# The stage between second attention and the expert choice, redone: 128-row projection, gate weights stationary, masks on two engines, experts' remainders spread

## The chip, the cores and the metric

One NeuronCore of one Trainium2 chip runs the whole program. The metric is the device time in microseconds (us) of one execution, and the number compared is the median over runs.

## What is computed

Two gated layers over x, 8 batches of 128 rows of 512 numbers, all in float32. The lines that matter here are the end of the second attention and the second feed-forward part, a mixture of 8 experts of which each row takes its best 2:

```python
out = jnp.einsum('de,bew->bdw', Wo, o) + bo[:, None]      # o: 64 x 128 per patch, after gelu
out = out * masks
...
x = x + tanh(g_xattn[1]) * out
h = layernorm(x)
logits = h @ W_gate + b_gate                               # 512 -> 8 experts
_, top_idx = jax.lax.top_k(logits, 2)
y_all = relu(einsum('bsd,edh->bseh', h, W_e) + b_e)
y = take_along_axis(y_all, top_idx[..., None], axis=2).mean(axis=2)
x = x + tanh(g_ffn[1]) * y
```

## The kernel before

The kernel is written by hand, one instruction stream for each engine, with semaphores between them. Each engine runs its own stream strictly in order, and that order is fixed in the code. The loops run over the 8 batches (b = 0 to 7). The stage that the change touches lies between the second attention and the experts. In this document it is called the middle stage. It starts at about 800 us of the trace and ends when the selection `sel` is there, at 842.75 us.

For each batch b the middle stage does this:

- ScalarE: `gelu(b)` in place on `o_t[0:64, b]` (L866; for b = 7 straight from PSUM, L874).
- GpSimd: `masked(b)` multiplies `o_t[0:64, b]` by the mask (L626). Row 64 of `o_t` (loaded by L403) holds the mask itself, and row 64 of `wo1g` holds the bias.
- TensorE: `output(b)` is the projection, `wo1g` (65 x 128, stationary) times `o_t[:, b]` (65 x 512, moving), into PSUM bank 2 + b % 2 (L1670). float32 matmuls are two instructions each.
- VectorE: `attended(b)` adds it to X (L1210), then `bn_stats` (L911) and `bn_aggr` (L914).
- GpSimd: `row_scale(3, b)`, three short instructions, makes the row's scale (L496 to L499).
- VectorE: `final_rows(b)` normalises the rows into `h` (L917), one or two batches later. SyncE stores them (`keep_rows`, L449). For b of 4 and more, `final_rows` waits until the first four stores have landed, since the buffers are used again.
- TensorE: `turn_last(b)`, four transposes of `h` (L1677). ScalarE: copies them to `xt` (L877).
- TensorE: `gate(b)` (L1683), with `xt` (128 x 128) stationary and `wg` (128 x 8) moving, for four k.
- VectorE: `choose(0)` for batches 0 to 3 and `choose(1)` for 4 to 7 (L1240 to L1255) make `sel`. Ahead of them it copies `tri` (L1233).

TensorE's order is `output` 0, 1, 2, and then for i = 3 to 10: `output(i)`, `turn_last(i-3)`, `gate(i-4)`. Behind `sel` come the lists of rows for each expert, the gather of rows by an indirect DMA, and 23 tiles of expert matmuls (`expert(i)`). Each expert's weights are split into a high part (`expert_hi`, ScalarE, L683) and a remainder (`expert_lo`, GpSimd L502 or VectorE L1223), four pieces for each of 8 experts, 32 in all. Before the change GpSimd makes pieces 8 to 15 behind the last `row_scale`, and VectorE makes pieces 0 to 7 behind the lists. Pieces 16 to 31 are made inside the experts' loop by both. `rows_lo(i)` (L1331) and `biased(i)` (L1338) are VectorE's other work there.

SyncE's queue loads experts 4 to 7 (L407) as soon as `ot_mm` counts the last `turn_out`, which is the turning of the attention's output (L1628), and after that it loads `route` and `tri_raw` (L452, L453), ahead of `keep_rows`.

Of the kernel before, what the change touches and what calls it, by code (L numbers as in the profile page):

```python
# [46 lines left out]
def flamingo_gated_two_layers(nc, x, ctx, ctx_t, mask_tq, mask_b, g_xattn, g_ffn, wq0, wk0, wv0, wo0,  # L47
# [6 lines left out]
    with ExitStack() as stack:  # L54
# [70 lines left out]
        wo1g = sb("wo1g", [E1 + 1, P])  # L125
# [124 lines left out]
        o_t = sb("o_t", [E1 + 1, B, D])  # L250
# [71 lines left out]
        HALF = N // 2  # L322

# [14 lines left out]
        def _(sp):  # L338
# [64 lines left out]
            sp.dma_start(o_t[E1:E1 + 1, :, :], mask_b.rearrange("b o d -> o b d")).then_inc(maskb_in, 16)  # L403
# [47 lines left out]
            sp.wait_ge(gelu_ok, CREDIT + B)  # L451
            sp.dma_start(route[:, :], c_route[:, P:]).then_inc(route_in, 16)  # L452
            sp.dma_start(tri_raw[:, :], c_route[:, 0:P]).then_inc(route_in, 16)  # L453
# [30 lines left out]
        def _(gp):  # L484
# [180 lines left out]
        def _(ac):  # L665
# [237 lines left out]
        def _(ve):  # L903
            start_counts(ve, (wo1_ok, ctl_ok, prep_v, cap_ok, stat_ok, aggr_ok, h_ok, htl_ok, rot_ok, e_ok, rec_ok, at_ok, al_ok,
                              x1_ok, bbg_ok, lg_ok, lgm_ok, lgs_ok, lgi_ok, al2_ok, zw_ok, tb_ok, hc_ok, keep_ok, pen_ok, qk_ev,
                              cv_ok, mx_ok, sb_ok, oi_ok, on_ok, x3_ok, sel_ok, rank_ok, td_ok, x4_ok, real_ok, wel_v, tri_ok,
# [270 lines left out]
            for b in range(2, B):  # L1177
                mix(b, b % 2, last=b == B - 1)
                row_stats(2, b - 2, b % 2, x2_ok)
                if b == 3:  # L1180
                    nc.vector.tensor_scalar(wo1g[:, :], wo1[:, :], tanh_g[0:E1 + 1, 1:2], None, ALU.mult).then_inc(wo1_ok, 1)
# [6 lines left out]
                if b == B - 5:  # L1188
                    ve.wait_ge(maskb_in, 16 * (B + 1))
# [42 lines left out]
            ve.wait_ge(route_in, 32)  # L1232
            nc.vector.tensor_copy(tri[:, :], tri_raw[:, :]).then_inc(tri_ok, 1)  # L1233

            def choose(half):
# [4 lines left out]
                nc.vector.tensor_tensor(gl[:, at, :], ps[:, 4 + half, 0:4 * EX].rearrange("p (b e) -> p b e", b=4),  # L1240
# [122 lines left out]
        def _(pe):  # L1363
# [441 lines left out]
```

## Time and profile before

| | us |
|---|---|
| median of 3 runs (962.52 to 968.63) | 965.4 |
| the profiled execution, whole | 966.84 |
| its span in the trace | 965.0 |
| granted TensorE clock, mean over the span | 0.952 of full |
| TensorE matmuls busy in the span | 894.5 (93%) |
| VectorE, ScalarE, GpSimd busy | 619.6, 325.0, 404.5 |
| middle stage, 801.2 to 842.75 | 41.55 |

Times inside the kernel are read from the trace of the one profiled execution, in us from the start of its span. The 1.84 us between its span and its whole time lie around the span. A granted clock of 1.00 is 2.4 GHz and 0.50 is 1.2 GHz.

### The profile page before, as it was taken

The page shows a single profiled execution, that of the slowest core. Times are in us where ns is not written, and L with a number is a line of the kernel's source. Part 1 is how long each engine was busy: PE and PEld are TensorE (multiplying, and loading weights), DVE is VectorE, ACT ScalarE, POOL GpSimd, SP SyncE. Part 2 cuts the span into 40 slices and gives each one's busy share as a digit, 9 for nine tenths or more (in the row PEclk, how much of TensorE's full clock was granted, in tenths as well). Part 3 has the DMA queues.
Part 4 walks back from the last instruction along what each step waited for, and adds up shares of the span by engine and source line. Part 5 has one row for each costly group of instructions (what it writes and reads, how often), then busy time and mean ns, then how long its engine had stood idle before and what let it go on. Part 6 is the DMA issues. An engine that isn't in the chain of part 4 may idle for free.

```text
span 965.0 us, 13870 instructions
## 1 busy us (share of the span) xinstructions
PE 894.5 (93%) x4771; PEld 728.3 (75%) x4771; DVE 619.6 (64%) x1067; ACT 325.0 (34%) x581; POOL 404.5 (42%) x417
## 2 busy tenths in 40 slices
PE   5999999999999999999999999988999998857993
PEld 4778878978878877877977877865888885745772
DVE  5975675375674276575376577578888875777345
ACT  4333143223133214124214124221665664612230
POOL 4651532251442153253153153337764606528551
PEclk9999999999999999999999999989999996559997
DMA  9020120020120011120011011202344205313448
GB/s 314 11 88 1 33 88 1 12 87 2 33 88 1 13 45 43 33 88 1 12 43 44 1 27 52 87 26 61 113 136 134 66 2 214 142 44 131 134 149 307
DMA packets 42242, 70.13 MB, mean 73 GB/s; under 512 B 7034, under 2 KB 14779, under 8 KB 42051
## 3 DMA queue, kind: packets, MB, share of 16 engines
q1 hardware_dynamic: 37060, 56.97, 18.1%
q0 software_dynamic: 3680, 12.06, 3.8%
q8 instruction: 43, 0.70, 0.3%
q10 hardware_dynamic: 1440, 0.24, 0.1%
q14 instruction: 19, 0.16, 0.1%
HBM read 52.61 MB, written 10.22 MB: 65 GB/s over the span
## 4 chain that ended last, share of the span: by engine, by line
PE 84%; DVE 8%; issue 3%; DMA 2%; ACT 1%; ACTq 1%; POOL 1%; DVEq 0%; SPq 0%
PE ps L1370 18%; PE ps L1372 18%; PE ps L1371 17%; PE ps L1491 6%; PE ps L1483 6%; PE ps L1620 5%; PE ps L1499 3%; PE ps L1608 3%; PE ps L1601 2%; PE ps L1670 1%; DMA rows_in<-h_rows,gather_i 1%; PE ps L1716 1%; PE ps L1628 1%; DVE h L917 1%; PE ps L1576 1%
## 5 line engine op out<-in xcount | busy, mean ns | idle before, releaser
L528 POOL TENSOR_TENSOR q_t<-rot_a,rot_b 128x512 f32<-128x512 f32 x64 | 82.7, 1291 | 152.8 <-DVE rot_b L962 152.8
L960 DVE TENSOR_TENSOR rot_a<-ps,cos 128x512 f32<-128x512 f32 x80 | 55.2, 689 | 87.2 <-PE ps L1372 86.6
L1370 PE MATMUL ps<-xt_hi,wq_hi 128*128 128x512 f32 x256 | 107.6, 420 | 0.5 <-DVE rot_b L962 0.5
L1370 PE MATMUL ps<-wo_hi,at_hi 128*128 128x512 f32 x256 | 106.7, 417 | 0.4 <-DVE at_lo L1068 0.4
L1372 PE MATMUL ps<-xt_hi,wq_lo 128*128 128x512 f32 x256 | 101.1, 395 | 0.0
L1371 PE MATMUL ps<-xt_lo,wq_hi 128*128 128x512 f32 x256 | 101.0, 394 | 0.0
L1372 PE MATMUL ps<-wo_hi,at_lo 128*128 128x512 f32 x256 | 100.2, 391 | 0.0
L1371 PE MATMUL ps<-wo_lo,at_hi 128*128 128x512 f32 x256 | 99.9, 390 | 0.0
L755 ACT ACTIVATE ps<-ps 128x512 f32<-128x512 f32 x64 | 37.2, 582 | 178.6 <-PE ps L1483 178.6
L768 ACT ACTIVATE at_hi<-ps 128x512 fp32r<-128x512 f32 x64 | 38.2, 597 | 171.7 <-PE ps L1499 171.7
L1073 DVE TENSOR_TENSOR X<-ps,X 128x512 f32<-128x512 f32 x64 | 44.2, 690 | 74.0 <-PE ps L1372 73.7
L592 POOL TENSOR_TENSOR k_blk<-k,diag 96x512 fp32r<-96x512 f32 x64 | 65.4, 1053 | 24.7 <-DMA k<-qk_lo 24.7
L502 POOL TENSOR_TENSOR wq_lo<-wq_raw,wq_hi 128x512 fp32r<-128x512 f32 x32 | 41.4, 1297 | 78.8 <-ACT wq_hi L683 78.8
L1370 PEld LDWEIGHTS ps<-wo_hi,at_hi 128*128 128x128 f32 x256 | 48.0, 187 | 30.3 <-DVE at_lo L1068 17.2
L1491 PE MATMUL ps<-v_ones,e_w 128*128 128x129 f32 x512 | 67.7, 275 | 0.0
L528 POOL TENSOR_TENSOR k_t<-rot_a,rot_b 128x512 f32<-128x512 f32 x16 | 20.7, 1294 | 108.5 <-DVE rot_b L962 108.5
L1620 PE MATMUL ps<-v_pad,p_t 128*128 128x72 f32 x512 | 64.8, 269 | 1.1 <-ACT p_t L836 1.0
L1068 DVE TENSOR_TENSOR at_lo<-ps,at_hi 128x512 fp32r<-128x512 f32 x64 | 44.2, 690 | 32.6 <-ACT at_hi L768 32.6
L1483 PE MATMUL ps<-q_t,k_t 128*128 128x512 f32 x128 | 64.1, 593 | 0.0
L1491 PEld LDWEIGHTS ps<-v_ones,e_w 128*128 128x128 f32 x512 | 62.8, 192 | 0.7
L1620 PEld LDWEIGHTS ps<-v_pad,p_t 128*128 128x128 f32 x512 | 62.2, 192 | 1.4 <-ACT p_t L836 1.1
L1051 DVE TENSOR_TENSOR e_w<-ps,cap 128x512 f32<-128x512 f32 x64 | 44.1, 689 | 28.8 <-ACT ps L757 28.5
(217 smaller groups left out, 2131.2 us busy)
## 6 DMA issues: line engine op xcount, KB each, us to landing
wq_raw<-in_wq SPq DMA_DIRECT2D x8, 1024.0 KB, 5.2
wo_raw<-in_wo SPq DMA_DIRECT2D x8, 1024.0 KB, 5.1
w_raw<-in_we SPq DMA_DIRECT2D x8, 1024.0 KB, 5.7
X<-in_x SPq DMA_DIRECT2D x4, 512.0 KB, 11.9
wk_raw<-in_wk SPq DMA_DIRECT2D x8, 256.0 KB, 2.9
q_t<-in_ctx_t SPq DMA_DIRECT2D x2, 1024.0 KB, 9.5
wv_raw<-in_wv SPq DMA_DIRECT2D x4, 512.0 KB, 3.7
ctx_s<-in_ctx SPq DMA_DIRECT2D x8, 256.0 KB, 4.2
```

The source lines that it names most:

```text
L528: nc.gpsimd.tensor_tensor(dst, rot_a[:, r % 2, :], rot_b[:, r % 2, :], ALU.add).then_inc(rope_ok, 1)
L592: nc.gpsimd.tensor_tensor(k_blk[0:PARTS, b % 2, g, patch, :, :], bcast(k3[0:PARTS, g, patch * P:(patch + 1) * P].bitcast(F32), HG), diag[0 ...
L960: nc.vector.tensor_tensor(heads(rot_a[:, r % 2, :]), heads(bank), bcast(cos[:, :], 4), ALU.mult)
L1051: nc.vector.tensor_tensor(heads(e_w[:, b % 2, :]), heads(ps[:, 2 + b % 2, :]), bcast(cap[:, :], G), ALU.min).then_inc(e_ok, 1)
L1068: nc.vector.tensor_tensor(at_lo[:, b % 2, :], ps[:, 6, :], at_hi[:, b % 2, :].bitcast(F32), ALU.subtract).then_inc(al_ok, 1)
L1073: nc.vector.tensor_tensor(X[:, b, :], ps[:, 7, :], X[:, b, :], ALU.add).then_inc(x1_ok, 1)
L1370: nc.tensor.matmul(dst, w_hi, x_hi, start=start and k == 0, stop=False)
L1371: nc.tensor.matmul(dst, w_hi, x_lo, start=False, stop=False)
L1372: last = nc.tensor.matmul(dst, w_lo, x_hi, start=False, stop=stop and k == n - 1)
L1483: nc.tensor.matmul(ps[:, 2 + b % 2, :], k_t[:, b * P:(b + 1) * P], q_t[:, :, b * P:(b + 1) * P], start=True, stop=True).then_inc(s_mm, 1)
L1491: last = nc.tensor.matmul(ps[:, 4 + n // 2, at:at + P + 1], e_w[:, b % 2, n * P:(n + 1) * P], v_ones[:, b, 1 if odd else 0, 0:P + 1], star ...
L1620: last = nc.tensor.matmul(ps[:, 6 + j, patch * VA:(patch + 1) * VA], p_t[:, u % 2, n * P:(n + 1) * P], v_pad[:, at:at + VA], start=head == ...
```

## The change

- `wo1g` and `o_t` have 128 rows instead of 65. Rows 65 to 127 of `wo1g` are zeros (rows 64 to 127 by a memset, then row 64 is written over), and the mask is loaded into rows 64 to 127 of `o_t`, as 64 copies, 1 MB, later in SyncE's queue than the one row was.
- Gate: `wg` (8 columns) is stationary and `xt` (128 columns) moves. The result, 8 x 128, is copied to SBUF by ScalarE (`gate_row`) and turned back by TensorE (`gate_columns`).
- Masks 0, 1, 5 and 6 are made by VectorE, masks 2, 3, 4 and 7 by GpSimd.
- TensorE issues `output(0)` and `output(1)` ahead of the last `turn_out`.
- The order of GpSimd's stream: masks 2 to 4, then `row_scale(0)` to `row_scale(7)` with six `expert_lo` (pieces 0 to 5) and `masked(7)` between them. VectorE makes pieces 6 to 11 behind the lists and 12 to 15 behind the first `rows_lo`.
- ScalarE makes six high parts ahead of the loop and one or two in each of its rounds. The copy of `tri` moves from VectorE to ScalarE.
- `route` and `tri_raw` are loaded during the second attention, and no longer between the experts' loads and `keep_rows`.

```diff
-        wo1g = sb("wo1g", [E1 + 1, P])
+        wo1g = sb("wo1g", [P, P])
-        o_t = sb("o_t", [E1 + 1, B, D])
+        o_t = sb("o_t", [P, B, D])
+        BY_VECTOR = (0, 1, 5, 6)
+        def masks_done(b):
+            return sum(n <= b for n in BY_VECTOR), sum(n <= b for n in range(B) if n not in BY_VECTOR)
...
-            sp.dma_start(o_t[E1:E1 + 1, :, :], mask_b.rearrange("b o d -> o b d")).then_inc(maskb_in, 16)
...
+                if b == 2:
+                    sp.dma_start(o_t[E1:P, :, :], mask_b.rearrange("b o d -> o b d").to_broadcast([P - E1, B, D])).then_inc(pen_raw, 16)
                 stack(b)
...
+            for g in range(2):
+                sp.wait_ge(k3_in[g], 48 * B)
+                sp.wait_ge(q3_in[g], 48 * B)
+            sp.dma_start(route[:, :], c_route[:, P:]).then_inc(route_in, 16)
+            sp.dma_start(tri_raw[:, :], c_route[:, 0:P]).then_inc(route_in, 16)
             sp.wait_ge(ot_mm, CREDIT + B)
...
-            masked(0)
-            masked(1)
-            for b in range(2, B):
+            for b in range(2, 5):
                 masked(b)
-                if b == B - 1:
-                    nc.gpsimd.memset(ones_r[:, :].bitcast(F32), 1.0).then_inc(kz_ok, 1)
-                row_scale(3, b - 2, b % 2)
-            row_scale(3, B - 2, 0)
-            row_scale(3, B - 1, 1)
-            for n in range(2 * KT, 4 * KT):
-                expert_lo(n // KT, n % KT)
+            nc.gpsimd.memset(ones_r[:, :].bitcast(F32), 1.0).then_inc(kz_ok, 1)
+            for b in range(B):
+                row_scale(3, b, b % 2)
+                if b == 1:
+                    masked(B - 1)
+                elif b < B - 1:
+                    expert_lo(*divmod(b - min(b, 1), KT))
...
+            def gate_row(b):
+                ac.wait_ge(ot_mm, CREDIT + B + b + 1)
+                nc.scalar.activation(r_d[0:EX, b // 4, b % 4 * P:(b % 4 + 1) * P], ps[0:EX, 4 + b % 2, 0:P], ACT.Copy).then_inc(ot_ev, 1)
...
+            for n in range(6):
+                expert_hi(n // KT, n % KT)
             for b in range(B):
                 ac.wait_ge(ht_mm, CREDIT + 2 * B + b + 1)
                 nc.scalar.activation(xt[:, :, b * P:(b + 1) * P], heads(ps[:, b % 2, :]), ACT.Copy).then_inc(hth_ok, 1)
-                for n in range(2 * b, 2 * b + 2):
+                if b >= 1:
+                    gate_row(b - 1)
+                if b == B - 1:
+                    gate_row(b)
+                for n in range(6 + b + min(b, 2), 7 + b + min(b + 1, 2)):
                     expert_hi(n // KT, n % KT)
+            ac.wait_ge(route_in, 32)
+            nc.scalar.activation(tri[:, :], tri_raw[:, :], ACT.Copy).then_inc(tri_ok, 1)
...
+                    nc.vector.memset(wo1g[E1:P, :], 0.0).then_inc(wo1_ok, 1)
+                    ve.wait_ge(wo1_ok, CREDIT + 1)
...
+            masked(0)
+            masked(1)
             over_sums(B - 1, 1)
+            masked(5)
+            masked(6)
...
-            for n in range(KT + 2):
+            for n in range(6, 12):
                 expert_lo(n)
             rows_lo(0)
-            expert_lo(KT + 2)
-            expert_lo(KT + 3)
+            for n in range(12, 16):
+                expert_lo(n)
...
-                    last = nc.tensor.matmul(ps[:, 4 + b // 4, b % 4 * EX:(b % 4 + 1) * EX], xt[:, k, b * P:(b + 1) * P], wg[:, k, :],
+                    last = nc.tensor.matmul(ps[0:EX, 4 + b % 2, 0:P], wg[:, k, :], xt[:, k, b * P:(b + 1) * P],
                                             start=k == 0, stop=k == KT - 1)
-                last.then_inc(gate_mm, 1)
+                last.then_inc(ot_mm, 1)
+
+            def gate_columns(b):
+                pe.wait_ge(ot_ev, CREDIT + B - 1 + b + 1)
+                nc.tensor.transpose(ps[:, 6 + b // 4, b % 4 * EX:(b % 4 + 1) * EX], r_d[0:EX, b // 4, b % 4 * P:(b % 4 + 1) * P],
+                                    ident[0:EX, 0:EX]).then_inc(gate_mm, 1)
...
-            for b in range(3):
-                output(b, b % 2)
+            output(0, 0)
+            output(1, 1)
+            turn_out(B - 1, 1)
+            output(2, 0)
             for b in range(3, B + 3):
                 if b < B:
                     output(b, b % 2)
                 turn_last(b - 3)
                 if b >= 4:
                     gate(b - 4)
+                if b >= 5:
+                    gate_columns(b - 5)
             gate(B - 1)
+            gate_columns(B - 2)
+            gate_columns(B - 1)
```

## Rows read from the trace of the kernel before

**Rows 1.** Windows: window, its length, busy time of each engine, PEclk, DMA share, GB/s

```profile
812.00:829.00 17.00, 17.00 (x58) 12.39 (x56) 9.44 (x20) 7.75 (x15) 8.17 (x17) 0.50 0.47 178
838.50:858.20 19.70, 5.64 (x25) 5.48 (x25) 16.00 (x48) 6.59 (x13) 5.18 (x5) 0.50 0.34 124
```

**Rows 2.** Timeline of one round: start, us, engine, line, operation, tiles, count, idle before

```profile
820.56 2.05 PE L1670 MATMUL ps<-o_t,wo1g 65*128 65x512 f32 x2
822.41 1.06 PE L1677 MATMUL ps<-ident,h 128*128 128x128 f32 x4
822.65 0.69 DVE L1210 TENSOR_TENSOR X<-ps,X 128x512 f32<-128x512 f32 x1 [2.20 <-PE ps L1670]
823.26 1.71 PE L1683 MATMUL ps<-wg,xt 128*128 128x8 f32 x8
823.38 0.69 DVE L911 BATCH_NORM_STATS2 stats<-X 128x6 f32<-128x512 f32 x1
824.11 0.18 DVE L914 BATCH_NORM_AGGREGATE mean_var<-stats 128x2 f32<-128x6 f32 x1
824.22 0.55 DVE L917 TENSOR_SCALAR h<-X,mean,rstd 128x512 f32<-128x512 f32 x1
824.83 2.05 PE L1670 MATMUL ps<-o_t,wo1g 65*128 65x512 f32 x2
```

**Rows 3.** Windows in which the clock falls, stays low, is low and rises, or stays full

```profile
801.25:801.50 0.25, 0.25 (x2) 0.25 (x3) 0.00 (x0) 0.25 (x1) 0.25 (x1) 0.59 0.00 0
803.20:808.40 5.20, 5.20 (x6) 1.65 (x6) 3.03 (x6) 0.55 (x1) 1.52 (x4) 0.50 0.74 246
671.60:675.10 3.50, 3.37 (x8) 2.13 (x9) 3.40 (x8) 0.64 (x2) 0.93 (x4) 0.51 0.34 86
675.00:675.25 0.25, 0.25 (x3) 0.17 (x2) 0.25 (x1) 0.16 (x1) 0.25 (x2) 1.00 0.78 197
883.25:888.00 4.75, 2.23 (x11) 1.43 (x10) 4.70 (x5) 1.17 (x3) 4.09 (x5) 1.00 0.42 145
```

**Rows 4.** Timeline, the float32 matmul that fills half of the stretch from 671.6

```profile
672.29 1.91 PE L1576 MATMUL ps<-h,wqk 128*128 128x512 f32 x2
```

**Rows 5.** Timeline, the head of the middle stage

```profile
798.72 3.71 POOL L626 TENSOR_TENSOR o_t<-o_t,mask_bb 64x512 f32<-64x512 f32 x3 [25.23 <-ACT o_t L866]
799.03 3.22 ACT L866 ACTIVATE o_t<-o_t 64x512 f32<-64x512 f32 x6
799.18 1.11 PE L1620 MATMUL ps<-v_pad,p_t 128*128 128x72 f32 x8 [0.97 <-ACT p_t L836]
801.20 1.92 PE L1628 MATMUL ps<-ident,o_n 128*64 128x128 f32 x8 [0.91 <-DVE o_n L1152]
805.16 0.69 DVE L1210 TENSOR_TENSOR X<-ps,X 128x512 f32<-128x512 f32 x1 [4.02 <-PE ps L1670]
```

**Rows 6.** Timeline, the tail of the middle stage

```profile
829.87 10.80 POOL L502 TENSOR_TENSOR w_lo<-w_raw,w_hi 128x512 fp32r<-128x512 f32 x8
829.93 1.49 DVE L917 TENSOR_SCALAR h<-X,mean,rstd 128x512 f32<-128x512 f32 x1 [0.44 <-POOL rstd L499]
831.34 1.29 DVE L1233 CAST tri<-tri_raw 128x128 fp32r<-128x128 f32 x1
839.39 0.18 DVE L1240 TENSOR_TENSOR gl<-ps,bg 128x32 f32<-128x32 f32 x1
842.57 0.18 DVE L1255 TENSOR_SCALAR sel<-rank 128x32 fp32r<-128x32 f32 x1
```

**Rows 7.** One line of the source each: duration min/median/max in ns, when, shapes

```profile
L1424 PE MATMUL ps<-maskf,ones x2: 275/275/275, 23.6 to 23.7; 128*128 128x128 f32 x2
L877 ACT ACTIVATE xt<-ps x8: 597/597/597, 812.4 to 835.1; 128x512 f32<-128x512 f32 x8
```

**Rows 8.** Timeline, VectorE and SyncE's queue where `wo1g` and the mask rows are made ready

```profile
637.04 0.70 DVE L1181 TENSOR_SCALAR wo1g<-wo,tanh_g 65x128 f32<-65x128 f32 x1
676.32 0.52 SPq L397 DMA_DIRECT2D ctx_s<-in_ctx  x1
683.87 2.60 SPq L421 DMA_DIRECT2D k<-qk_hi  x4
```

More of the change, by code:

```diff
@@ L449, in keep_rows @@
                 sp.dma_start(h_rows[b * P:(b + 1) * P, :], (h if b % 4 < 2 else h2)[:, b % 2, :]).then_inc(hrow_out, 16)
-            sp.wait_ge(gelu_ok, CREDIT + B)
-            sp.dma_start(route[:, :], c_route[:, P:]).then_inc(route_in, 16)
-            sp.dma_start(tri_raw[:, :], c_route[:, 0:P]).then_inc(route_in, 16)
             for b in range(B):
@@ L679, in _ @@
             start_counts(ac, (ot_ev, gates_ok, hth_ok, cth_ok, wkh_ok, wvh_ok, wqh_ok, wo_hi_ok, v_ok, th_ok, ex_ok, ah_ok, wbh_ok,
-                              lge_ok, zt_ok, qkh_ok, p_ok, pt_ok, gelu_ok, weh_ok, r_ok, gh_ok))
+                              lge_ok, zt_ok, qkh_ok, p_ok, pt_ok, gelu_ok, weh_ok, r_ok, gh_ok, tri_ok))
             def hi_part(dst, raw, done):
@@ L905, in _ @@
                               x1_ok, bbg_ok, lg_ok, lgm_ok, lgs_ok, lgi_ok, al2_ok, zw_ok, tb_ok, hc_ok, keep_ok, pen_ok, qk_ev,
-                              cv_ok, mx_ok, sb_ok, oi_ok, on_ok, x3_ok, sel_ok, rank_ok, td_ok, x4_ok, real_ok, wel_v, tri_ok,
+                              cv_ok, mx_ok, sb_ok, oi_ok, on_ok, x3_ok, sel_ok, rank_ok, td_ok, x4_ok, real_ok, wel_v,
                               slot_ok, hot_ok, glo_ok, y0_ok))
@@ L1180, in _ @@
                 if b == 3:
-                    nc.vector.tensor_scalar(wo1g[:, :], wo1[:, :], tanh_g[0:E1 + 1, 1:2], None, ALU.mult).then_inc(wo1_ok, 1)
+                    nc.vector.memset(wo1g[E1:P, :], 0.0).then_inc(wo1_ok, 1)
+                    ve.wait_ge(wo1_ok, CREDIT + 1)
+                    nc.vector.tensor_scalar(wo1g[0:E1 + 1, :], wo1[:, :], tanh_g[0:E1 + 1, 1:2], None, ALU.mult).then_inc(wo1_ok, 1)
                     nc.vector.memset(q3[PARTS:PARTS + 1, :, :, :].bitcast(F32), 1.0).then_inc(pen_ok, 1)
@@ L1188, in _ @@
                 if b == B - 5:
-                    ve.wait_ge(maskb_in, 16 * (B + 1))
+                    ve.wait_ge(maskb_in, 16 * B)
                     rows(0, 0, p_w)
@@ L1204, in _, with masked @@
                 batch(b, b % 2, more=b + 2 < B, last=b == B - 1)
+            def masked(b):
+                ve.wait_ge(gelu_ok, CREDIT + b + 1)
+                nc.vector.tensor_tensor(o_t[0:E1, b, :], o_t[0:E1, b, :], mask_bb[0:E1, b, :], ALU.mult).then_inc(keep_ok, 1)
+            masked(0)
+            masked(1)
             over_sums(B - 1, 1)
+            masked(5)
+            masked(6)
             def attended(b, j):
@@ L1231, in _ @@
             final_rows(B - 1, 1)
-            ve.wait_ge(route_in, 32)
-            nc.vector.tensor_copy(tri[:, :], tri_raw[:, :]).then_inc(tri_ok, 1)
             def choose(half):
@@ L1239, in choose @@
                 ve.wait_ge(gate_mm, CREDIT + 4 * half + 4)
-                nc.vector.tensor_tensor(gl[:, at, :], ps[:, 4 + half, 0:4 * EX].rearrange("p (b e) -> p b e", b=4),
+                nc.vector.tensor_tensor(gl[:, at, :], ps[:, 6 + half, 0:4 * EX].rearrange("p (b e) -> p b e", b=4),
                                         bcast(bg[:, :], 4), ALU.add).then_inc(rank_ok, 1)
@@ L1663, in _ @@
             weighted(B - 1, 1, H1 - 1)
-            turn_out(B - 1, 1)
             def output(b, j):
-                pe.wait_ge(om_ok, CREDIT + b + 1)
+                by_v, by_p = masks_done(b)
+                pe.wait_ge(keep_ok, CREDIT + B + by_v)
+                if by_p:
+                    pe.wait_ge(om_ok, CREDIT + by_p)
                 pe.wait_ge(x3_ok, CREDIT + b - 1)
@@ L1719, in parts_done @@
             def parts_done(i):
+                if i == 0:
+                    return 0, KT
                 if i < 4:
-                    return min(i + 1, 2) * KT, max(i - 1, 0) * KT
+                    return 2 + (i - 1) * KT, 6
                 if i < EX - 1:
-                    return 2 * KT + 2 * (i - 3), 2 * KT + 2 * (i - 3)
-                return 2 * KT + 9, 2 * KT + 7
+                    return 10 + 2 * (i - 3), 6 + 2 * (i - 3)
+                return 19, 13
             def expert(i):
@@ L1730, in expert @@
                     by_v, by_p = parts_done(i)
-                    pe.wait_ge(wel_v, CREDIT + by_v)
-                    if by_p:
-                        pe.wait_ge(wel_ok, CREDIT + by_p)
+                    pe.wait_ge(wel_ok, CREDIT + by_p)
+                    if by_v:
+                        pe.wait_ge(wel_v, CREDIT + by_v)
                 pe.wait_ge(glo_ok, CREDIT + i + 1)
```

3 lines of the change are left out of this document (2 added, 1 removed).

## The prediction

> **What bounds the kernel now.** I read the windows of the middle stage first, then the timeline of one round, then the windows of TensorE's clock, and last the head and the tail of the stage. In the windows, TensorE is busy for 17.00 of 17.00 us between 812 and 829, and its clock is at the lower level, 1.2 GHz, all that time [rows 1]. VectorE is busy for 9.44, ScalarE and GpSimd for less. So in the rounds TensorE sets the pace, and it does so at half speed. The timeline shows a round of 4.27 us (820.56 to 824.83): from start to start 1.85 for the projection's two instructions, 0.85 for four transposes and 1.57 for the eight gate instructions [rows 2]. (Starts are used, since the durations shown include a tail that overlaps the next instruction.) VectorE waits 2.20 us in each round for the projection.
>
> The clock falls at 801.3 [rows 3]. Before it TensorE had been idle 0.97 us for `p_t` and 0.91 us for `o_n`, with 1.11 us of narrow matmuls between [rows 5]. Then it streams the 65-row projection without a gap from 803.2 to 808.4, 5.20 of 5.20 us, and the clock doesn't rise. At 671.6 to 675.0 it was low as well, and there it rose, after no more than 3.5 us in which TensorE was busy for 3.37 [rows 3]. Half of that stretch was a float32 matmul of 512 columns over 128 rows, 1.91 us [rows 4], and the rest 97-row matmuls and transposes. So busy time of 65 rows did not raise the clock and less busy time of 97 and 128 rows did. Between 883.25 and 888.0 TensorE was busy only 2.23 of 4.75 us, with 128 rows throughout, and the clock stayed full [rows 3]. In the rounds 1.57 of each 4.27 us are spent on gate instructions of 8 columns, in which TensorE mostly loads weights.
>
> At the end of the stage, VectorE's short instructions run beside GpSimd's eight remainders, 10.80 us in a row. `h` takes 1.49 us instead of 0.55, `tri` takes 1.29, and from the end of `h`(7) at 831.42 to the end of `sel` at 842.75 it is 11.33 us [rows 2, 6].
>
> **The change, part by part.** The sum is made on the end of `sel`, since what stands behind it (lists, gather, 23 tiles) keeps its order.
>
> *Projection of 128 rows, gate weights stationary.* At either clock the two instructions of the projection stream 512 columns as before: nothing saved by the shape itself. The gate becomes eight instructions that move 128 columns. The trace has one float32 matmul of that shape, two instructions of 275 ns each, tail included, at the full clock [rows 7]. Lower bound for the spacing: a transpose of 128 columns, a quarter of 0.85 at the lower clock [rows 2], so 107 ns at the full one. Upper bound: 275. I take the lower, as the tails overlap in rows 2 too: 8 x 107 ns, or 0.85, for a gate at the full clock and 1.71 at the lower. Now it is 1.57. `gate_columns` adds one small transpose, about 0.11 or 0.2. A round of TensorE is then half of 1.85 + 0.85, and 0.85 + 0.11, so 2.3 us at the full clock, and 4.27 + 0.14 + 0.2 or some 4.5 at the lower. (The projection's 1.85 holds 0.14 of waiting, so 4.4 is nearer, and is used.)
>
> *Which clock.* Moving columns through all 128 rows now fill projection, transposes and gate. At the lower clock that is nearly all of 4.4 us, like the stretch that rose at 675. At the full clock and VectorE's pace (below) it is 2.2 of 2.6 us, more than the 2.23 of 4.75 that kept it. I take the full clock for the rounds. Whether it falls at the head doesn't matter much: `output(0)` and `output(1)` now fill the 0.91 us gap, and if it falls all the same, TensorE streams `output(1)`, `turn_out` and `output(2)`, 1.7 + 1.9 [rows 5] + 1.7 us at the lower clock, which takes it to about 809, no later than VectorE's third addition.
>
> *Head.* ScalarE's gelus end at 799.6, 800.1, ... 802.25 (3.22 us for six) [rows 5]. GpSimd's masks take 3.71/3 = 1.24 us [rows 5]. VectorE does masks 0 and 1 before it is wanted for `o_n`. Masks 5 and 6 stand ahead of `attended(0)` in its stream, and GpSimd's masks 2 to 4 run from 800.2 to 803.9. A VectorE mask alone costs 0.69 (an addition of as many elements, [rows 2]) and beside GpSimd up to 1.49 (`h`, [rows 6]). So from 801.75, when gelu 5 is done, they end between 803.2 and 804.8. I take 804.5 for the start of `attended(0)`, against 805.16 now [rows 5]. Bounds: 803.2 to 805.5.
>
> *Rounds.* VectorE needs 0.69 + 0.69 + 0.18 us and gaps, 1.57 from start to the end of the group [rows 2]; with 0.14 to the next (an estimate) it is 1.7, and with `h` 2.25. Two rounds without `h` put `attended(2)` at 807.9. Five more lead to `attended(7)`. In each GpSimd now runs a `row_scale` (about 1.0 us, an estimate from three short instructions) and one remainder or mask of 1.24 to 1.35 [rows 5, 6]. GpSimd needs 2.4 us a round, so it is not far from setting the pace, and beside its long instruction `h` takes up to 1.49 in place of 0.55. I take a third of that, 0.3, as the mean: 2.6 a round (bounds 2.25 and 3.2), 13.0 for five, `attended(7)` at 820.9. Then come 1.7 and three `h` of 0.55: `h`(7) ends at 824.2 against 831.42, so 7.2 us earlier. `h`(4) also waits for the first four stores, which are now issued closer to it; the store of `h`(3) leaves at 818.6 and `h`(4) is due at 820.3, so a stall of 0 to 1 is inside the bounds.
>
> *Tail.* GpSimd has no remainder left, and `tri` is on ScalarE. `choose(1)` takes 3.36 us from 839.39 to 842.75 now, of which its second instruction alone stood beside GpSimd [rows 6]; without about 1.0 of this it is 2.4. `choose(0)` needs as much and runs while TensorE and ScalarE turn the last batch. From the end of `h`(7): transposes 0.65, `xt` 0.6 [rows 7], gate 1.1 behind gate 6, `gate_row` 0.3, `gate_columns` 0.3, `choose(1)` 2.4, together 5.35 against 11.33 now. Saved: 6.0. (Bounds of this saving: 4.0 if the clock is low there and each step costs 0.3 more, 6.5.)
>
> *Behind it.* TensorE waits between few matmuls from 838.5 to 858.2 at the lower clock, busy 5.64 of 19.70 [rows 1]. Its waits are as long after the change, so I take nothing there. VectorE makes four remainders behind the first `rows_lo` instead of two, in the shadow of the first tile: 0 to 1 us, I take 0. The pieces 0 to 5 that GpSimd makes early are not on VectorE's path now either, since the first tile waits for the gather. ScalarE's six high parts ahead of the loop end at about 807.3, and `xt`(0) is wanted after 810. `route` and `tri_raw` are loaded while the DMA queues are idle.
>
> *Ahead of it.* The memset of 64 rows of `wo1g` with its wait stands in front of VectorE's 0.70 us `wo1g` instruction [rows 8]. There VectorE is on the path (TensorE waits for VectorE a few instructions later). The row of the same size is 0.18 to 0.70; I take 0.3 lost. The 1 MB of mask rows goes out behind the load at 676.32. The next waiting work of SyncE comes at 683.87 [rows 8], 7 us later, which hides it; without that cover it would delay the keys of batch 2 by some 3 us.
>
> Sum: 7.2 + 6.0 - 0.3 = 12.9 us. The profiled execution took 966.84 us, its span is 965.0, so this gives a span of 952.1 and 953.9 whole. The profiled run is 1.4 above the median of 965.4, so for the median it is **952.5 us**.
>
> **The rivals.**
>
> *No change, the clock stays low in the rounds.* The gate's stationary operand has only 8 columns, and the trace doesn't show whether such a matmul counts like a wide one. If it does not, little has changed. TensorE then needs 4.4 us a round: `turn_last(0)` at 810.4 behind `h`(0), the ten steps up to gate 7 at 839.5, `gate_row` and `gate_columns` until 840.3, `choose(1)` until 842.7. That is today's 842.75. With the memset it makes **965.5**. For it: 5.20 us without a gap did not raise the clock. Against it: those had 65 rows.
>
> *Half of it.* The clock rises and falls again in turn. Rounds then are on average midway between 2.6 and 4.4, so 3.5: five rounds cost 4.5 more, and the tail about 1: **958**. Here the Trainium skill has a rule that would lead there. "TensorE: Matmul & The Clock Gate", section "Part 4: PE-mode transpose", says that transposes don't count as work that keeps the clock up. By that rule the 0.43 us of each round would fall out of the count. No row here tells it apart, as transposes never stand alone long enough.
>
> *Slower.* The gate's matmuls are dearer than I take them. At the upper bound of 275 ns a piece, eight are 2.2 us at the full clock instead of 0.85 and TensorE needs 3.6 a round, which still is less than today's 4.27. It decides only with the low clock: 550 ns a piece make a round of 7.1, and eight rounds cost 22 us: 987. The point from which it is slower by over 1% is a spacing of about 360 ns at the low clock, where 213 is seen for 128 columns.
>
> **How the numbers follow.** Full clock in the rounds: 0.60. By the bounds above (head -1.3 to +1.0, rounds -1.75 to +3, tail -0.5 to +2) its own range is 949 to 958. Half of it: 0.15. No change: 0.21. Slower: 0.04. The range 948 to 965.5 takes in the first two and half of the third. For this kernel 1% is 9.7 us, about what a measurement can tell from no change. Faster by over 1% (below 955.7) needs the first case and nine tenths of it, plus a little of the second: 0.57. Slower by over 1%: 0.04. Within 1%: 0.39.
>
> **What would show it.** In the profile after: PEclk near 1.0 from about 805 to 825; two L1670-like projection instructions 0.43 us apart; VectorE's additions 2.3 to 2.9 us apart and waiting little for TensorE; gate instructions 107 ns apart; the last `sel` at about 830, followed by TensorE's clock at 0.50 until the first tiles. `attended(0)` near 804.5 with one or both masks stretched. If the clock is 0.50 in the rounds, the forecast is wrong at the step "which clock". If the rounds take over 3.2 us at the full clock, the step on GpSimd and VectorE is wrong. If `sel` is early and the end is not, something behind `sel` gives it back.

## The result and the profile after

| | before | after |
|---|---|---|
| median, us | 964.1 (960.47 to 968.63, 6 executions) | 957.17 (956.29 to 961.09, 6 executions) |
| ratio of the two, 95% interval | | 0.9928 (0.9899 to 0.9956) |
| profiled execution, us (its span) | 966.84 (965.0) | 957.5 (955.7) |
| mean granted clock, profiled execution | 0.952 | 0.971 |
| end of the last `sel`, us | 842.75 | 832.76 |
| end of `h`(7), us | 831.42 | 824.91 |

Forecast were 952.5 us and a range of 948 to 965.5. The kernel is 0.7% faster, a little over half of the 1.3% that were forecast (965.4 to 952.5): between the forecast's likeliest case and no change, and by size at the rival called "half of it" (958). The range was wide, since its upper end was the time of the rival "no change". Faster by over 1%, to which the forecast gave 0.57, did not come true; within 1%, to which it gave 0.39, did.

The windows of the middle stage in the kernel after, to be read against [rows 1]. The columns are the window, its length, busy time of PE (TensorE), PEld (its weight loads), DVE (VectorE), ACT (ScalarE) and POOL (GpSimd), PEclk (the granted clock), DMA share, GB/s:

```profile
801.50:804.10 2.60, 0.02 (x1) 0.00 (x0) 2.56 (x4) 2.54 (x5) 1.50 (x2) 1.00 0.43 120
804.10:812.00 7.90, 5.96 (x10) 2.23 (x11) 7.23 (x13) 2.58 (x6) 6.96 (x15) 0.55 1.00 375
812.00:815.00 3.00, 3.00 (x14) 1.74 (x12) 2.00 (x4) 0.86 (x3) 2.47 (x5) 0.50 1.05 406
815.00:829.00 14.00, 13.35 (x88) 8.51 (x89) 9.42 (x21) 8.95 (x20) 7.13 (x13) 1.00 0.35 131
```

TensorE is idle for 2.58 of 2.60 us, its clock then falls (at 804.9) and is low until about 815.1, and from there on it is full, until the last gate is done. So the rounds up to `attended(5)` (816.12) run for the most part at the low clock, and the two behind it at the full one. The head, which holds that gap:

```profile
798.13 0.69 DVE L1229 TENSOR_TENSOR o_t<-o_t,mask_bb 64x512 f32<-64x512 f32 x1 [0.32 <-ACT o_t L877]
798.58 1.93 PE L1698 MATMUL ps<-o_t,wo1g 128*128 128x512 f32 x4
798.69 4.17 POOL L635 TENSOR_TENSOR o_t<-o_t,mask_bb 64x512 f32<-64x512 f32 x3 [26.20 <-ACT o_t L877]
800.21 3.20 DVE L1229 TENSOR_TENSOR o_t<-o_t,mask_bb 64x512 f32<-64x512 f32 x2 [0.61 <-ACT o_t L877]
803.34 0.67 DVE L1239 TENSOR_TENSOR X<-ps,X 128x512 f32<-128x512 f32 x1
804.16 1.35 PE L1698 MATMUL ps<-o_t,wo1g 128*128 128x512 f32 x2 [2.63 <-DVE X L1239]
```

The two projections at 798.58 are done early. But VectorE is in masks 5 and 6, 3.20 us beside GpSimd's masks instead of 2 x 0.69, and `attended(0)`, for which `output(2)` waits, starts only at 803.34. Of the two gaps in the kernel before [rows 5] the one of 0.97 us for `p_t` is still there (ahead of 797.63), the one of 0.91 us is filled by the two projections, and a new one of 2.63 us, from 801.5 to 804.16, is longer than both together.

A round at the full clock, against [rows 2]:

```profile
819.07 1.04 PE L1711 MATMUL ps<-xt,wg 128*8 128x128 f32 x8
820.03 0.22 PE L1717 MATMUL ps<-ident,r_d 8*128 8x8 f32 x1
820.19 1.12 PE L1698 MATMUL ps<-o_t,wo1g 128*128 128x512 f32 x2
820.31 0.55 DVE L936 TENSOR_SCALAR h<-X,mean,rstd 128x512 f32<-128x512 f32 x1
821.15 0.60 PE L1705 MATMUL ps<-ident,h 128*128 128x128 f32 x4
821.35 0.69 DVE L1239 TENSOR_TENSOR X<-ps,X 128x512 f32<-128x512 f32 x1 [0.49 <-PE ps L1698]
821.68 1.04 PE L1711 MATMUL ps<-xt,wg 128*8 128x128 f32 x8
```

From gate to gate it is 2.61 us where [rows 2] has 4.27. TensorE still sets the pace: it works without a gap from 819.07 to 821.68, and VectorE waits 0.49 us for it. And the tail, against [rows 6]:

```profile
824.36 0.55 DVE L936 TENSOR_SCALAR h<-X,mean,rstd 128x512 f32<-128x512 f32 x1 [0.44 <-POOL rstd L508]
825.23 0.66 PE L1705 MATMUL ps<-ident,h 128*128 128x128 f32 x4
826.94 0.66 PE L1705 MATMUL ps<-ident,h 128*128 128x128 f32 x4
828.65 1.04 PE L1711 MATMUL ps<-xt,wg 128*8 128x128 f32 x8
830.31 0.19 DVE L1267 TENSOR_TENSOR gl<-ps,bg 128x32 f32<-128x32 f32 x1 [2.52 <-PE ps L1717]
832.58 0.18 DVE L1282 TENSOR_SCALAR sel<-rank 128x32 fp32r<-128x32 f32 x1
```

`h`(7) is ready at 824.91, yet its transposes start at 826.94: TensorE first works off batches 5 and 6, 1.71 us each. VectorE waits 2.52 us for the last gate.

### The profile page after: what moved, and what is told of

It is laid out like the page before. It is cut to its first block, busy times and chain, and to the rows that moved or that the text cites. A ratio compares the mean times of both kernels' runs of the same rounds, so it can differ in the third digit from the quotient of the medians.

```text
span 955.7 us, 13899 instructions
## 1 busy us (share of the span) xinstructions
PE 882.6 (92%) x4779; PEld 715.1 (75%) x4779; DVE 619.2 (65%) x1073; ACT 327.4 (34%) x590; POOL 397.1 (42%) x411
## 4 chain that ended last, share of the span: by engine, by line
PE 79%; DVE 9%; DMA 4%; issue 3%; POOL 2%; ACT 2%; ACTq 0%; DVEq 0%; SPq 0%
PE ps L1397 17%; PE ps L1399 16%; PE ps L1398 16%; PE ps L1518 6%; PE ps L1510 6%; PE ps L1647 5%; PE ps L1526 3%; PE ps L1635 3%; PE ps L1628 2%; DMA rows_in<-h_rows,gather_i 1%; DMA rb<-in_router_b 1%; POOL y_rows L655 1%; DVE stats L930 1%; DVE h L936 1%; POOL w_lo L511 1%
```

## The experiments

All are compared with the kernel before on the same chip; for the kernel after that were six executions with a median of 964.1, the 76 of the first line are those beside the experiments. "Clock" is the mean granted TensorE clock of each timed execution; the last two columns say which part is there.

| kernel | median us | ratio (95%) | clock, lowest to highest | rows | gate |
|---|---|---|---|---|---|
| before (76 executions) | 963.1 | 1 | 0.952 to 0.964 | 65 | old |
| after | 957.17 | 0.9928 (0.9899 to 0.9956) | 0.969 to 0.974 | 128 | standing |
| e1 | 959.91 | 0.9962 (0.9936 to 0.9988) | 0.959 to 0.973 | 65 | standing |
| e2 | 957.65 | 0.9936 (0.9911 to 0.9961) | 0.961 to 0.973 | 128 | old |
| e3, order of before | 958.36 | 0.9954 (0.9930 to 0.9978) | 0.966 to 0.971 | 128 | old |
| e5 | 963.72 | 1.0011 (0.9995 to 1.0026) | 0.956 to 0.961 | 65 | old |
| e9, order of before | 961.49 | 0.9988 (0.9972 to 1.0003) | 0.963 to 0.969 | 65 | standing |
| e6 | 959.63 | 0.9967 (0.9951 to 0.9983) | 0.968 to 0.975 | 128 | standing |
| e4 | 956.17 | 0.9920 (0.9896 to 0.9944) | 0.970 to 0.975 | 128 | standing |
| e7 | 955.07 | 0.9926 (0.9901 to 0.9950) | 0.972 to 0.978 | 128 | standing |
| e8 | 954.31 | 0.9914 (0.9896 to 0.9933) | 0.973 to 0.976 | 128 | standing |
| e10 | **950.48** | **0.9873 (0.9850 to 0.9896)** | 0.972 to 0.980 | 128 | standing |
| e11 | 953.88 | 0.9911 (0.9888 to 0.9934) | 0.972 to 0.978 | 128 | standing |
| e12 | 955.53 | 0.9920 (0.9892 to 0.9947) | 0.963 to 0.971 | 128 | old |

### What raises the clock: e1, e2, e3, e5, e9

e1, the kernel after with 65 rows:

```diff
-        wo1g = sb("wo1g", [P, P])
-        o_t = sb("o_t", [P, B, D])
+        wo1g = sb("wo1g", [65, P])
+        o_t = sb("o_t", [65, B, D])
...
```

> The kernel after, with 65 rows of weights and outputs instead of 128 in the projection (same 512 columns, same result). Theory 'rows' (streaming all 128 rows raises and keeps TensorE's clock): PEclk 0.50 through the rounds, attended additions 4.2 to 4.5 us apart as before the change, sel at 840 to 843, the whole about 964 to 966, or 7 to 9 us over the kernel after (957.2). Rival 'contention' (the gain is VectorE and ScalarE freed of GpSimd's remainders and of the old order, the clock only follows): the rounds keep the pace of 2.6 to 3.0 us and the whole stays within 956 to 959. Rival 'gate' (the gate's eight 128-column instructions lift the clock, the rows of the projection don't matter): PEclk rises once gates begin (about 814), the whole 957 to 960.

e2, the kernel after with the old gate:

```diff
-                    last = nc.tensor.matmul(ps[0:EX, 4 + b % 2, 0:P], wg[:, k, :], xt[:, k, b * P:(b + 1) * P],
+                    last = nc.tensor.matmul(ps[:, 6 + b // 4, b % 4 * EX:(b % 4 + 1) * EX], xt[:, k, b * P:(b + 1) * P], wg[:, k, :],
...
-                    gate_row(b - 1)
...
-                    gate_columns(b - 5)
...
```

> The kernel after, but the gate again with the attended rows stationary and 8 columns moving; no copy of its row, no transposes back; projection still 128 rows. Theory 'rows': projection and transposes alone keep the clock at full in the rounds, and the tail is shorter by the row copy and the columns: 954 to 957.5. Rival 'gate' (the 8-column form is time that doesn't keep the clock): PEclk 0.50 in the rounds, a round of TensorE 4.3 us, sel near 840, the whole 962 to 966.

e3, the kernel before with the rows alone:

```diff
-        wo1g = sb("wo1g", [E1 + 1, P])
-        o_t = sb("o_t", [E1 + 1, B, D])
+        wo1g = sb("wo1g", [P, P])
+        o_t = sb("o_t", [P, B, D])
...
+                    nc.vector.memset(wo1g[E1:P, :], 0.0).then_inc(wo1_ok, 1)
...
```

> The kernel before with one part of the change: projection over 128 rows (with the memset and the mask rows that it needs), old order, old gate, old masks and remainders. Theory 'rows': the clock rises in the rounds and they go at the pace of VectorE and GpSimd (2.6 to 3.0 us instead of 4.27): h(7) 6 to 9 us earlier, but the tail of GpSimd's eight remainders keeps its 10.8 us beside choose; the whole 957 to 960 against 964.1 before. Rival 'gate': the clock stays at 0.50 from 812 to 829 and the whole is 964 to 966. Rival 'contention': at most 1 us gained.

e5, both edits of e1 and e2 at once:

> The kernel after with both edits undone that give TensorE other work in the rounds: 65 rows in the projection and the gate with 8 columns moving; the new order, masks and remainders stay. Over the runs so far the mean granted clock and the time move together, about 0.75 us per 0.001; after had 0.969 to 0.974, before 0.952 to 0.964, and 65 rows alone fell into two groups, 0.959 to 0.964 and 0.970 to 0.973. Theory 'clock' (each of the two edits makes it likely that the clock comes back in the rounds, together they make it certain): no run above 0.965, PEclk 0.50 all through the rounds, 962 to 965. Rival 'contention' (order, masks and remainders bring the gain themselves): 957 to 960 at whatever clock.

e9, the kernel before with the edit of e2 the other way round (the standing gate alone):

> The kernel before with the standing gate alone (eight instructions that move 128 columns, row copy, transposes back); projection still 65 rows, old order, masks and remainders. e1 (65 rows in the kernel after) showed two groups of clocks, e5 (65 rows and the old gate) none above 0.961. Theory 'each part lifts the clock by itself, the gate less surely than the rows': clocks in two groups as in e1, some at 0.955 to 0.96 and some at 0.965 to 0.97, median 959 to 963. Rival 'the gate form lifts nothing without the rows or the new order': all clocks 0.952 to 0.964 like before, and the dearer gate makes it 964 to 966.

The rounds in e3, then in e5, both as windows with the columns above:

```profile
801.00:805.00 4.00, 4.00 (x9) 1.78 (x8) 1.17 (x2) 0.68 (x2) 0.28 (x1) 0.65 0.44 128
805.00:809.00 4.00, 1.85 (x4) 0.30 (x2) 3.83 (x9) 0.00 (x0) 3.49 (x8) 1.00 1.00 367
813.00:817.00 4.00, 4.00 (x24) 2.60 (x25) 3.46 (x8) 3.06 (x6) 4.00 (x9) 1.00 1.01 382
817.00:821.00 4.00, 3.53 (x26) 2.61 (x23) 3.53 (x8) 2.60 (x5) 1.23 (x5) 1.00 0.36 135
```

```profile
813.00:817.00 4.00, 4.00 (x15) 2.86 (x14) 1.74 (x5) 1.37 (x4) 2.26 (x4) 0.50 0.71 273
817.00:821.00 4.00, 4.00 (x15) 2.86 (x14) 1.77 (x4) 1.02 (x2) 2.26 (x4) 0.50 0.17 66
821.00:825.00 4.00, 4.00 (x15) 2.86 (x15) 1.78 (x5) 1.11 (x2) 2.30 (x4) 0.50 0.19 70
```

With the rows of the projection alone, in the old order (e3), the clock falls as before, during `turn_out`, but is back at 803.8, after some 2 us of 128-row projections, where the kernel before stayed low through 5.20 us of 65-row ones [rows 3]. It is full in the rounds, all nine executions are at 0.966 or more, and by the ratios two thirds of the gain are there (0.46 of 0.72%, 4.7 us by the medians; the intervals overlap, so the share is rough). Theory "rows" held there, and in e2 nearly (957.65, its range ended at 957.5). The median of e1, 959.91, lies in the range of its rival "gate". With neither part but everything else of the change (e5) TensorE is busy for 4.00 of 4.00 us at 0.50, as in [rows 1], the rounds are 4.27 us again (`attended` at 816.05, 820.32), no execution is above 0.961, and the gain is nil. The theory "clock" held: without the clock the rest of the change gains nothing. In its trace the stage is shorter, 42.52 us from the start of the first gelu to the end of `sel` for 44.73 before, but the part behind `sel` is longer (124.8 us for 122.3); why isn't shown. The rival "contention" alone falls.

Each part can do it by itself, less surely. e1 falls into two groups: six executions at 0.959 to 0.964 take 960.9 to 966.4 us, six at 0.970 to 0.973 take 954.8 to 958.9. Its profiled execution is of the second kind (the first kind has no trace), and its clock rose at 812.6, just behind the first eight gate instructions (PEclk is 0.50 from 812.2 to 812.45):

```profile
810.60 1.88 PE L1711 MATMUL ps<-xt,wg 128*8 128x128 f32 x8
812.40 1.22 PE L1698 MATMUL ps<-o_t,wo1g 65*128 65x512 f32 x2
814.00 1.04 PE L1711 MATMUL ps<-xt,wg 128*8 128x128 f32 x8
```

Eight gate instructions take 1.88 us, the next eight 1.04. e2 ranges over both groups; in its trace the clock is low from about 810.5 to 817.3. e9 did not show two groups: its clocks, 0.963 to 0.969, lie in between, and its interval reaches past 1. Yet its trace shows what the standing gate does alone. The clock rises at 812.5, near the end of the first gates (811.20 to 812.81), and is full behind them:

```profile
809.00:813.00 4.00, 4.00 (x15) 1.95 (x14) 2.76 (x6) 2.06 (x5) 3.49 (x8) 0.56 1.06 400
813.00:817.00 4.00, 4.00 (x22) 2.25 (x22) 2.40 (x5) 3.13 (x7) 2.63 (x6) 1.00 0.46 175
```

The last rounds are 2.62 and 2.61 us, and from the first gelu to the end of `sel` it is 40.04 us (38.15 in e3, 44.73 before). That the median gains only some 2 us of this fits that the profiled execution is the fastest of its twelve; the rest isn't explained. So my theory "rows" in e1 was wrong as put (65 rows do not pin the clock), and so was "gate" for half of the executions. With the two parts together it came back every time: all six executions of the kernel after are at 0.969 or more, and of the 88 of before and e5 none is above 0.964.

### Remainders: e6

```diff
                 if b == 1:
                     masked(B - 1)
-                elif b < B - 1:
-                    expert_lo(*divmod(b - min(b, 1), KT))
+            for n in range(2 * KT, 4 * KT):
+                expert_lo(n // KT, n % KT)
...
```

> The kernel after, but GpSimd makes its remainders as before the change: none between the row scales, eight in a row behind the last one; VectorE has six ahead of the gathered rows and two behind. Theory 'contention': h(6), h(7) and the router's instructions stretch beside GpSimd as before, from the end of h(7) to the end of sel 10 to 11.5 us instead of 7.85, partly won back by lighter rounds: 959 to 961.5. Rival 'TensorE sets the tail' (it works off turns and gates at 1.71 us a batch, VectorE has slack there): 957 to 958.5.

Measured 959.63, 2.5 above the kernel after (3.7 by the ratios), "contention" right. In its tail GpSimd is busy in one piece, and the router's instructions are three times and more as long as the 0.42 of the kernel after:

```profile
819.85 10.94 POOL L511 TENSOR_TENSOR w_lo<-w_raw,w_hi 128x512 fp32r<-128x512 f32 x8
819.91 1.49 DVE L936 TENSOR_SCALAR h<-X,mean,rstd 128x512 f32<-128x512 f32 x1 [0.44 <-POOL rstd L508]
821.53 1.27 DVE L1272 TENSOR_TENSOR rank_b<-gl 128x256 f32<-128x256 f32 x1
822.72 1.49 DVE L1273 TENSOR_TENSOR rank_a<-gl 128x256 f32<-128x256 f32 x1
832.68 0.39 PE L1741 MATMUL ps<-sel,ones_r 128*128 128x64 f32 x1 [6.86 <-DVE sel L1282]
```

From the end of `h`(7) to the end of `sel` it is 11.14 us (7.85 after), while `attended(7)` comes 15.53 us behind `attended(0)` instead of 18.01: part of the tail is won back in the rounds. The spread is thus worth 2.5 to 3.7 us once the clock is full. In e5, where TensorE was at half speed, it brought little: VectorE's instructions were short, but it waited 5.53 us for the last gate, and the tail was 10.33 us. The Trainium skill states a rule that would make this, "SBUF — State Buffer", section "SBUF: two separate sides": a VectorE instruction with two SBUF inputs and a GpSimd instruction that reads SBUF share a pair of ports, the one that starts first has it for the whole instruction, and the other blocks. The rows agree: 1.27 and 1.49 us are about the length of one GpSimd remainder, 10.94 / 8 = 1.37.

### Masks: e4 and e7

```diff
             over_sums(B - 1, 1)
-            masked(5)
-            masked(6)
...
+            masked(5)
             for b in range(2, B):
                 attended(b, b % 2)
+                if b == 2:
+                    masked(6)
```

> The kernel after, but VectorE makes mask 5 behind attended(1) and mask 6 behind attended(2), not both ahead of attended(0). Theory 'gap' (the two masks ahead of attended(0) keep TensorE idle from 801.5 to 804.2, the clock falls there, and the first rounds are 3 to 3.8 us instead of 2.6): attended(0) at 801.7 to 802.5, no wait over 1 us on TensorE there, PEclk over 0.9 from 801 on, sel 2 to 4 us earlier, the whole 953 to 955.5. Rival 'pace' (GpSimd or VectorE set the rounds anyway, and the masks are only moved from ahead of the rounds into them): 956.5 to 958.

```diff
-        BY_VECTOR = (0, 1, 5, 6)
+        BY_VECTOR = ()
...
```

> The kernel after, but all eight masks on GpSimd (five ahead of the row scales, 5 to 7 in the first three rounds, six remainders behind in the later ones). Theory 'gap' (the two VectorE masks ahead of attended(0) cost more than they give): attended(0) 1.5 to 2 us earlier, less idle time of TensorE at 801 to 804, 955 to 957. Rival 'split' (1.24 us a mask on GpSimd sets the pace of the first rounds, h is stretched): rounds of 3 us, 958 to 960.

e4 took 956.17, above the range of "gap" and below that of "pace"; e7 took 955.07, in that of "gap". In e7 `attended(0)` starts at 797.60, 3.36 us behind the start of the first gelu (6.87 in the kernel after), TensorE's clock stays full from 800 to 812, and `attended(5)` comes 14.30 us behind the start of the first gelu (19.65 after). So VectorE's half of the masks, a part of the change, costs 3.5 us at `attended(0)` and 5.3 at `attended(5)`. But most of it is given back at once: to the end of `sel` 1.8 us are left of it in both traces (34.46 in e4 and 34.45 in e7, from the first gelu, for 36.29), by the medians 1 and 2.1 us, by the ratios next to nothing (0.9920 and 0.9926 against 0.9928). The waits of VectorE between 797 and 830 in e7 (engine, line, for what: us in total, times, longest):

```profile
DVE h L937 <- DMA h_rows<-h: 3.0, 1, 3.0
DVE gl L1264 <- PE ps L1714: 2.7, 2, 2.3
```

`h`(4) takes the buffer of `h`(0) and waits until the first four rows are stored, and the stores run beside 4 MB of expert weights (DMA share 1.04 from 812 to 815). This is the stall that the forecast had named with 0 to 1 us. In the kernel after it is nil, in e7, where the rounds are earlier, 3.0, and the clock fell behind it, at 816.

### The stores: e8 and e10

e8 is e4 with the loads of experts 6 and 7 behind the stores of `h`(1) and `h`(3):

> The kernel of e4 with one thing more: the loads of experts 6 and 7 (1 MB each) are issued behind the stores of h(1) and h(3), not ahead of all stores. In e4 VectorE stood 2.66 us ahead of h(4), released by the DMA of the h rows, and a round later TensorE's clock fell. Theory 'stores': that idle time falls below 0.5 us, attended(7) comes 15.3 to 16.5 us behind attended(0) instead of 18.7, 953 to 954.5 against 956.2 of e4. Rival 'pace': the wait only moves (to the row scales of GpSimd or to TensorE), 955.5 to 957.

e10 is e7 with

```diff
-            for e in range(FIRST, EX):
+            for e in range(FIRST, EX - 2):
                 load_expert(e)
...
             for b in range(B):
                 keep_rows(b)
+                if b in (4, 5):
+                    load_expert(b + 2)
```

> The kernel of e7 (all masks on GpSimd) with the loads of experts 6 and 7 issued behind the stores of h(4) and h(5). In e8 they stood behind the stores of h(1) and h(3), their transfers still ran beside the store of h(3), and VectorE waited 3.1 us ahead of h(4) as in e7. Theory 'stores': the stores 0 to 3 then run beside no load at their end, the wait goes, attended(7) comes 15.5 to 16.5 us behind attended(0) instead of 18.7, no clock dip in the rounds, 951.5 to 953.5 against 955.1 of e7. Rival 'pace': the store of h(3) takes some 3 us alone and the wait stays over 1.5 us, 954 to 956.

e8 missed its own cause: the wait was still 3.1 us. `h`(3) ended at 812.30, and its store landed 5.2 us after its issue. Two loads ran beside it, one issued at 807.86, which took 8.4 us to land, and one issued right behind the store, at 812.69; which of them held it up isn't shown. `attended(7)` came 18.98 us behind `attended(0)`. Only the time, 954.31, was as expected; by the ratios it is 0.6 us under e4, within the noise. In e10 no load is in flight beside the fourth store, which lands after 2.0 us:

```profile
DVE X L1238 <- PE ps L1697: 2.2, 3, 1.7
DVE h L939 <- DMA h_rows<-h: 0.4, 1, 0.4
```

The wait is 0.4 us, the median 950.48 (under the range of "stores"), 4.6 under e7, and 1.3% under before. It is the fastest of all kernels here, 5.3 us under the kernel after by the ratios and 6.7 by the medians. Its `attended(7)` was still 17.52 us behind `attended(0)`, over the 16.5 of my bound, as the clock of the profiled execution was low once from 807.35 (its mean, 0.972, is the lowest of its six; the others go to 0.980 and 948.5).

### The tail: e11 and e12

```diff
             for b in range(2, B):
+                if b >= 6:
+                    final_rows(b - 2, b % 2)
                 attended(b, b % 2)
-                final_rows(b - 2, b % 2)
+                if b < 6:
+                    final_rows(b - 2, b % 2)
```

> The kernel of e10 in which VectorE makes h(4) and h(5) ahead of attended(6) and attended(7), not behind. It tests the term that came out too small in the forecast: from the end of h(7) to the end of sel 7.85 us instead of 5.35, because TensorE still has the turns and gates of batches 5, 6 and 7 to do, 1.71 us each, when h(5), h(6) and h(7) come almost together. Theory 'backlog': with h(5) some 2 us earlier one batch is off the queue, from the end of h(7) to the end of sel 6.0 to 6.5 us, the whole 1 to 1.7 us under e10. Rival 'VectorE sets the tail' or 'h(5) delays attended(7) by as much': within 0.5 us of e10.

> The kernel of e10 with the gate again as before the change (attended rows stationary, 8 columns moving), 128 rows kept. Question: is the standing gate worth its row copy and transposes once the rounds run without a wait. Theory 'tail': from the end of h(7) to the end of sel 1 us less than in e10, as in e2 against after (6.89 against 7.85), clocks as in e10, 949 to 950.5. Rival 'gate keeps the clock': the 8-column time counts for less, the clock dips in the rounds in part of the runs as in e2 (some runs 0.970 or lower), 951.5 to 954.

e11: from the end of `h`(7) to the end of `sel` 5.88 us, as "backlog" has it, but nothing is gained: `h`(4) now waits for GpSimd ahead of `attended(6)`,

```profile
811.97 1.48 DVE L939 TENSOR_SCALAR h<-X,mean,rstd 128x512 f32<-128x512 f32 x1 [2.11 <-POOL rstd L510]
```

and from the first gelu to the end of `sel` it is 32.26 us against 32.29 in e10. So the backlog is real, and moving `h` only moves the wait. The expectation that the whole would be faster than e10 was wrong: the median is 3.4 above it. Why isn't shown. In the traces e11 is behind in the part behind `sel` (126.0 against 123.4 us), but 3.3 us ahead at the first gelu, and the trace of e10 is of its slowest execution.

e12: the rounds are as quick as they get (`attended(7)` 15.31 us behind `attended(0)`), but with the old gate the clock falls at the end of them, at about 816:

```profile
813.00:817.00 4.00, 3.17 (x25) 2.94 (x25) 3.65 (x6) 2.00 (x4) 4.00 (x9) 0.93 0.72 197
817.00:821.00 4.00, 4.00 (x21) 4.00 (x22) 3.46 (x5) 1.75 (x4) 3.11 (x3) 0.50 0.99 333
```

The tail is 7.28 us, not shorter than e10's 6.91, and all clocks are 0.963 to 0.971 where e10 has 0.972 to 0.980. "Gate keeps the clock" is right in direction and low in size: 955.53. With the standing gate the kernel is 4.5 to 5 us faster there. That these are lost where the clock falls isn't shown: from the first gelu to the end of `sel` the trace of e12 is even shorter than that of e10's slowest execution (31.67 against 32.29 us), and its part behind `sel` is longer (127.6 against 123.4).

## Why the forecast was right, and where it was off

- **The profiled pair and the medians.** In the traces the span is 9.3 us shorter, the medians differ by 6.9. Some of the pair's difference is luck ahead of the stage: the first gelu there starts at 796.47 instead of 798.02. In the kernel before the clock is low in a stretch around 645 to 652 (PEclk 0.56 over it), in the kernel after it is 1.00 there; both are low around 672 to 675. The trace of e9, whose code is that of the kernel before up to the stage, has 0.76 over 645 to 652 and starts the first gelu at 794.98, so 3 us of such a difference can come without any change. Of the 10.0 us by which `sel` is earlier, 1.55 are ahead of the stage and 8.4 in it; forecast were 13.2.
- **Ahead of it.** The forecast took 0.3 us as lost, and the traces show nothing lost. The memset takes 0.17 us, and the `wo1g` instruction behind it 0.34 instead of 0.70. The matmuls behind them start 0.29 later than before (642.58 for 642.29), but VectorE's instruction ahead of the memset is already 0.29 later (637.23 for 636.94). The 1 MB of mask rows costs nothing that shows: from SyncE's keys of one batch to those of the next it is 17.07 us in both traces.
- **Head.** Counted from the first gelu `attended(0)` is at 6.87, forecast 6.48: right, both masks stretched as said. What was wrong is the sentence that a fall of the clock in the head doesn't matter much. The gap of 2.63 us behind masks 5 and 6 lets it fall, and it stays low until 815.1.
- **Which clock.** Right as the forecast had it for the second half: 815 to 829 at 1.00, the last two rounds 2.62 and 2.61 us for a forecast 2.6. That the two numbers agree is luck in part. The forecast had VectorE at 2.25 with 0.3 for a stretched `h`, and TensorE at 2.3; in the trace `h` isn't stretched (0.52 and 0.55), and TensorE sets the pace with 2.62: 0.96 for the projection, 0.54 for the transposes, 0.97 for the gate and 0.15 for the columns, from start to start. The first rounds, 2.91, 2.99 and 3.83, ran at the low clock. The first of them would be no shorter without it: e2 has 2.91 and e3 2.89 there at the full clock, with `h`(0) stretched to 1.47 and 1.45 us beside GpSimd. Five rounds took 14.96 us, forecast 13.0. The argument was too simple in one point: it took 65-row streaming as unable to raise the clock, and e1 shows that with a gate of 128 moving columns it can.
- **The gate.** A matmul with 8 stationary columns was the open point on which "no change" stood (0.21). It is settled: gates at the full clock are 0.97 us from the first of eight to what follows (forecast 0.85), and they count for the clock (e1, e9, e12).
- **Tail, the mis-sized term.** Forecast 5.35, measured 7.85. The working took `turn_last(7)` straight behind `h`(7). It left out that `h`(5), `h`(6) and `h`(7) end within 1.45 us (823.46 to 824.91), and that TensorE needs 1.71 us of turn, gate and columns for each: `turn_last(7)` starts 2.03 us behind `h`(7), and the gates drift with it. The 2.4 for `choose(1)` is right (2.45). e11 bears the backlog out: with `h`(5) earlier the tail was 5.88.
- **Sum of the misses** in the stage: head +0.4, the two rounds behind it -0.35, five rounds +2.0, `attended(7)` to `h`(7) +0.3, tail +2.5, together 4.8 us. With 1.85 better ahead of it (the luck above, and 0.3 that was forecast as lost) and 0.7 worse behind it this is 3.6, the distance between 12.9 and 9.3.
- **Behind `sel`.** As forecast the lists run at the low clock with the same waits, and the first tile starts 9.15 us earlier than before, for 10.0 at `sel`: 0.8 was given back, partly since the DMA of the first gather landed 4.5 us after its issue instead of 3.65.
- **The rivals.** "Half of it" gave 958 from a clock that rises and falls in turn. The size came true, the mechanism did not: it fell once, from a gap on VectorE's side, and came back for the rest of the rounds and the gates. In the rival "no change" one sum is off: 4.27 + 0.14 + 0.2 is 4.61, not 4.5, so a round at the low clock would be 4.47 and not 4.4; the forecast itself doesn't rest on it. The Trainium skill's rule that transposes don't count ("TensorE: Matmul & The Clock Gate", section "Part 4: PE-mode transpose") is tested by none of these runs: the clock held in rounds with 0.54 us of transposes in 2.62, and nothing takes them out alone.

## What to carry to other kernels

Where an engine is at its lower clock, look first for what it does with few rows or few columns: filling a 65-row operand up to 128 rows with zeros cost nothing that shows and brought 4.4 to 4.7 us (e3), and a reordering that made the stage 2.2 us shorter in the trace (e5) returned nothing in the whole without it. Then look for the idle gap that lets the clock fall, and after each repair for the next wait, here masks, then stores behind loads, then TensorE's backlog. A load that is issued early only because its queue is free can hold up a store that is wanted.

## What was not expected of the hardware

- The time of one and the same kernel moves with the granted clock from execution to execution: over 76 executions of the kernel before from 0.952 (966.4 and 966.5 us) to 0.964 (957.6 to 959.6), by a straight line 0.62 us for each 0.001. The kernel after lies 0.013 higher by the mean and 5.9 us lower by the median. Half a per cent between two single executions of such a kernel says nothing by itself; look at their clocks too. Between kernels the line doesn't carry over: at their clocks it would put e9 some 4 us and e6 some 5 us lower than they are.
- Whether the clock comes back can differ from execution to execution of one kernel: e1 fell six to six, by the mean clock of the execution.
- A 256 KB store lands later beside 1 MB loads of the same queue: the fourth store landed 5.1 us after its issue in e7 and 5.2 in e8, with loads in flight, and after 2.0 in e10 and e12, without. The wait for it was 3.0, 3.1, 0.4 and 0.4 us.
